# A graph-attention kernel's weighted sums: one accumulator instead of two, a reduce for a copy, and spread-out source rows in the empty slots

## The reference

```
for i in range(3):                       # layer 0: three hops
    Hn = segment_sum(H[src] * edge_weight, dst) @ Wn[i].T + bn[i]
    H  = elu(Hn + H @ Ws[i].T + bs[i])   # no elu on the last
x = layernorm(x + H)

h = x @ W.T                              # layer 1: attention, 8 heads of 32
alpha = <h[src], a_src> + <h[dst], a_dst> + <relu(edge_attr @ edge_W.T + edge_b), h[dst]>
alpha = where(alpha >= 0, alpha, 0.2 * alpha)
ex = exp(alpha - segment_max(alpha, dst)[dst])
attn = ex / max(segment_sum(ex, dst)[dst], 1e-10)
x = layernorm(x + segment_sum(h[src] * attn, dst) + bias)
```

## Time and profile before

| | us |
|---|---|
| median of three runs | 3030.04 (3027.95 to 3031.69) |
| the profiled execution, its time | 3030.28 |
| its span in the trace | 3028.5 |
| DVE busy | 1797.2 (59%) |
| POOL busy | 1846.8 (61%) |
| PE busy | 2444.8 (81%) |
| indirect gathers on POOL (L636), 416 of them | 403.3 |
| adds to the two accumulators (L1830), 208 and 208 | 424 and 423 ns each at the median |
| exp columns (L1836), 104 of them | 169 / 684 / 1917 ns at least, median, most |

### The profile page before, as it was taken

One profiled execution on the slowest core, in us unless ns is written; L12 is line 12 of the kernel. 1 busy time (PEld: TensorE's weight loads), 2 busy tenths in 40 slices (PEclk: granted clock), 3 DMA queues, 4 the chain that ended last, 5 costly groups with the idle time before them and its releaser, 6 DMA issues.

```text
span 3028.5 us, 46970 instructions
## 1 busy us (share of the span) xinstructions
PE 2444.8 (81%) x9398; PEld 1573.7 (52%) x9399; DVE 1797.2 (59%) x4277; ACT 1068.3 (35%) x3018; POOL 1846.8 (61%) x1738
## 2 busy tenths in 40 slices
PE   6999976477777779999899999999776667727772
PEld 5888843255555544445444454445555555525552
DVE  7765559899999940001344401113777777768888
ACT  1222221488888830000000000000333333347773
POOL 4777777777777760000067777760677777747774
PEclk9999979699989999999999999998888888869997
DMA  3000010355555564443344444442577777757772
GB/s 128 3 4 3 3 25 3 112 183 183 183 183 183 183 208 132 135 129 112 101 124 122 122 123 132 133 138 86 176 217 217 216 218 219 212 122 215 207 210 82
DMA packets 425651, 415.44 MB, mean 137 GB/s; under 512 B 85386, under 2 KB 411489, under 8 KB 424929
## 3 DMA queue, kind: packets, MB, share of 16 engines
q1 hardware_dynamic: 367681, 348.28, 37.0%
q0 software_dynamic: 57888, 66.23, 9.8%
HBM read 247.08 MB, written 167.17 MB: 137 GB/s over the span
## 4 chain that ended last, share of the span: by engine, by line
PE 50%; POOL 14%; issue 11%; SPq 8%; DVE 6%; DMA 4%; DVEq 3%; ACT 2%; ACTq 0%; POOLq 0%
PE psum L912 27%; POOL gath L636 9%; SPq L489 6%; PE psum L724 5%; POOL rows_by_pair L597 5%; PE psum L1028 4%; DVEq L405 3%; PE psum L709 3%; PE psum L904 2%; DMA gath<-gat_rows,rec 2%; PE psum L783 1%; PE psum L842 1%; SPq L483 1%; PE psum L700 1%; ACT lw L1099 1%
## 5 line engine op out<-in xcount | busy, mean ns | idle before, releaser
L622 POOL DMA_INDIRECT rows_by_dst<-rec,place x392 | 381.1, 972 | 533.4 <-DVE place L1457 405.8
L912 PE MATMUL psum<-a_t,acc 128*128 128x512 f32 (+1 forms) x1400 | 553.7, 551 | 0.0
L636 POOL DMA_INDIRECT gath<-gat_rows,rec x416 | 403.3, 969 | 215.4 <-issue 116.2
L607 POOL DMA_INDIRECT rows_by_low_digit<-rec,place x392 | 438.0, 1117 | 127.6 <-issue 127.6
L842 PE MATMUL psum<-rhot,lw 128*128 128x256 f32 x1440 | 381.2, 419 | 160.1 <-ACT lw L1099 126.5
L597 POOL DMA_INDIRECT rows_by_pair<-rec,place x392 | 386.5, 986 | 161.5 <-issue 126.6
L842 PEld LDWEIGHTS psum<-rhot,lw 128*128 128x128 f32 x1440 | 276.5, 206 | 264.9 <-ACT lw L1099 163.7
L912 PEld LDWEIGHTS psum<-a_t,acc 128*128 128x128 f32 x1400 | 257.7, 195 | 271.7 <-issue 267.9
L1565 DVE SCALAR_TENSOR_TENSOR merged<-merged,same_of,psum 128x256 f32<-128x256 f32 x720 | 310.0, 477 | 30.5 <-PE psum L842 18.7
L912 PE MATMUL psum<-a_t,x 128*128 128x512 f32 (+1 forms) x700 | 294.3, 549 | 0.0
L1099 ACT ACTIVATE lw<-lhot,recs_pair 128x128 f32<-128x128 bf16 x720 | 236.8, 387 | 94.8 <-DVE lhot L1548 83.0
(11 more groups left out here) (319 smaller groups left out, 3464.7 us busy)
## 6 DMA issues: line engine op xcount, KB each, us to landing
a_t<-adjacency SPq DMA_DIRECT2D x450, 256.0 KB, 2.7
adjacency<-merged SPq DMA_DIRECT2D x721, 128.0 KB
gat_h_by_edge<-gath SPq DMA_DIRECT2D x104, 528.0 KB, 4.1
gath<-gat_h_by_edge SPq DMA_DIRECT2D x104, 528.0 KB, 4.0
gath<-gat_rows,rec POOLq DMA_INDIRECT x416
rows_by_pair<-rec,place POOLq DMA_INDIRECT x392
rows_by_low_digit<-rec,place POOLq DMA_INDIRECT x392
rows_by_dst<-rec,place POOLq DMA_INDIRECT x392
```

The lines of the kernel that those rows point to most:

```text
L607: pool.indirect_dma_start(out=rows_low, in_=rec[:, c, :], out_offset=bass.IndirectOffsetOnAxis(ap=place[:, 1, c:c + 1], axis=0), in_offset ...
L622: pool.indirect_dma_start(out=rows_dst, in_=rec[:, c, :], out_offset=bass.IndirectOffsetOnAxis(ap=place[:, 0, c:c + 1], axis=0), in_offset ...
L636: pool.indirect_dma_start(out=gath[:, g % 4, c % 4, :], out_offset=None, in_=hh_dram, in_offset=bass.IndirectOffsetOnAxis(ap=rec_i[:, c, 0 ...
L912: i = pe.matmul(sums[b], table_g[:, w, b * P:(b + 1) * P], a_t[:, q % NA, 0:width(g)], start=False, stop=w == USED - 1)
```

## The change

Three edits. First, `zeros` gets in word 0 of each record the number 18 times the partition plus the slot, by an iota on POOL after the clearing, and SP's prefilling waits for that as well. Empty slots of both tables then name differing sources. Second, `exp_columns` makes the same values by `tensor_reduce` with a maximum over an axis of length one, in place of `tensor_copy`. Third, all adds go to `acc`; each waits for the add right before it; the final addition of `x0` is gone, and so is POOL's clearing of `x0` with the wait for `s_end` in front of it. POOL's clearing of `acc` now stands first there, behind its own wait for `s_loc`.

```diff
+PAD_STEP = 18
...
-            sp.wait_ge(s_fill, 1)
+            sp.wait_ge(s_fill, 2)
             sp.dma_start(rows_pair.rearrange("(p c) k -> p (c k)", p=P), zeros[:, :]).then_inc(s_fill, 16)
...
             pool.memset(zeros[:, :], 0.0).then_inc(s_fill, 1)
-
-            pool.wait_ge(s_fill, 1 + 32)
+            pool.wait_ge(s_fill, 1)
+            pool.iota(zeros[:, :].bitcast(I32).rearrange("p (c k) -> p c k", k=REC)[:, :, 0], [[1, NS]], base=0,
+                      channel_multiplier=PAD_STEP).then_inc(s_fill, 1)
+
+            pool.wait_ge(s_fill, 2 + 32)
             pool.wait_ge(s_rec, 6)
...
-            pool.wait_ge(s_end, 64)
-            nc.gpsimd.memset(x0[:, :, :], 0.0).then_inc(s_clr, 1)
             pool.wait_ge(s_loc, LOCAL * NB)
             nc.gpsimd.memset(acc[:, :, :], 0.0).then_inc(s_clr, 1)
...
             def add(n, k, w):
                 dve.wait_ge(s_mm, n + 1)
-                if not (isinstance(n, int) and n < 2):
-                    dve.wait_ge(s_add, n - 1)
-                a = (acc, x0)[k % 2][:, bass.ds(w, 1), :].rearrange("p c d -> p (c d)")
+                if not (isinstance(n, int) and n == 0):
+                    dve.wait_ge(s_add, n)
+                a = acc[:, bass.ds(w, 1), :].rearrange("p c d -> p (c d)")
                 v.tensor_tensor(a, a, bank[k][:, 0:HX], ALU.add).then_inc(s_add, 1)
...
             def exp_columns(g, q, first):
                 if not first:
                     dve.wait_ge(s_mm, 4 * (g - 3))
-                v.tensor_copy(val[:, q, :, D:HX], s_sb[:, bass.ds(4 * g, 4), :]).then_inc(s_vx, 1)
+                v.tensor_reduce(val[:, q, :, D:HX], s_sb[:, bass.ds(4 * g, 4), :].unsqueeze(3), X,
+                                ALU.max).then_inc(s_vx, 1)
...
-            dve.wait_ge(s_clr, 2)
+            dve.wait_ge(s_clr, 1)
...
             dve.wait_ge(s_add, NC)
-            v.tensor_tensor(acc[:, :, :], acc[:, :, :], x0[:, :, :], ALU.add).then_inc(s_add, 1)
-            dve.wait_ge(s_add, NC + 1)
             v.tensor_scalar(x0[:, :, D:HX], acc[:, :, D:HX], 1e-10, None, ALU.max).then_inc(s_ln, 1)
```

More of the change, by code:

```diff
@@ L73 @@
 ROWS_STORED = 2 * (NG - 1)
+assert (P - 1) * PAD_STEP + NS <= N
 assert EC % PIECE == 0 and PIECE % 4 == 0 and 0 < LAST < EC and EC % U == 0 and SEGS * SEGC == EC and SEGS % 2 == 0 and SEGC % MID == 0
```

## The result

The changed kernel takes 3117.44 us (median of 4, 3116.81 to 3119.62) against 3030.86 us in the same measurement: a ratio of 1.0288 (95% interval 1.0275 to 1.0302). The forecast was 3116. The span of the profiled execution is 3115.8 us against 3028.5, 87.3 us more. Nearly all of the loss is in the weighted sums (98.9 us); the maxima lose 3.4 more, and the merge and the last gathers give 15 back.

The account below looks back on a forecast made before the run. In the sums DVE waits only for its sequencer, and the window-number load hides the long copy. +96 − 7.3 − 7.3 + 4.7 = +86 us on 3030.3 gives 3116 us, range 3084 to 3134.

Parts of the forecast that it names:

- The chained adds: Weighted sums on DVE: adds waiting for their predecessor start every 0.635 us instead of 0.34; +96 us.
- The step that made the number: DVE's sequencer between adds: wait release 0.04, register operation 0.07 later, add 0.10 later; 0.21 us behind the predecessor's end.
- The lower forms that were bounds (0.46, 0.57): Chained adds' spacing in us: 0.46 with wait nearly free (rival, 0.06), 0.57 if the register operation carries it (0.11).
- The long copy: Exp columns in the sums: window-number load of 1.84 us hides the copy, so reduce gains 0; contrary rival's chance 0.04.
- Merge and slots: Merge behind the last add gone, −7.3 us; differing sources in empty slots, last gather earlier, −7.3 us.
- The clearing: POOL's clearing of acc moves beside scans over the ends and delays a DVE operation on the path: +4.7 us.
- the two ends named: Bounds on the moved clearing's cost on the path: 0 and 5.9 us.
- that case (3.2): Moved clearing catches only DVE's operation at 2678.70, not the copy at 2676.03: it ends 3.2 us late.
- The iota: Start, on POOL before the prefilling: 0.7 to 0.9 us while DVE waits 1.75 for edges; 0, at most +0.9.
- the last rival: PE's clock falls in the sums: +38 us at most, 3154; 0 to 5 us at a third of the time; chance 0.07.

Follow-up runs that it names:

- chain_only: Kernel before with one accumulator, each add waiting for the one right before, no merge, clearings unmoved: 4358.44 us against 4267.04 on another chip, ratio 1.0204.
- wait_only: Kernel before, both accumulators and merge kept, each add waiting for the one right before: 4370.24 us against 4267.04 on another chip, ratio 1.0239.
- one_wait: Changed kernel with PE waited for once per quad, by its first add: 3102.83 us, ratio 1.0246 to the kernel before; sums 351.4 us.
- reduce_only: Kernel before with exp columns by a reduce, nothing else changed: 4265.01 us against 4267.04 on another chip, ratio 0.9992; sums 267.5 us.

## Why the prediction was right

*The chained adds.* The step that made the number was to count what the sequencer does between an add's end and the next one's start, and it held: 0.21 us predicted, 0.21 measured, in rows of three kernels (`chain_only`, `wait_only` and the changed one). The three steps are there one by one: behind the add that ends at 2864.767 the separate wait instruction comes at 2864.805, the register operation at 2864.874 and the add at 2864.978, so 0.04, 0.07 and 0.10 us, as the prediction had put them together.

The size was short. In the middle of the loop 16 chunks take 14.27 us instead of 10.38, 3.89 more and not 3.69. Of the 0.20 us, about 0.08 is that an add that is no longer overlapped takes 0.430 and not 0.424 us (0.642 a step and not 0.635); 0.02 lies behind a short copy; 0.10 lies behind the two loads, where the prediction had 0.04 less and each distance grew by 0.03 (medians 2.41 to 2.44, 2.80 to 2.83). Over 26 steps that would be 5 us more than forecast; it is 2.9, since the start of the sums loses less. The first 28 adds take 4.3 us more than before, where the loop's pace would give 6.8; about 1 us of that is the reduce's.

The lower forms that were bounds (0.46, 0.57) are real too: `one_wait` has the 0.57, since there the register operation alone carries the wait, and 0.46 is the distance from the last add to the instruction behind it. As to the rule of the Trainium skill, "VectorE: DVE Perf Modes", section "The DRAIN you can't avoid", that a semaphore costs nothing between chained operations, the trace disagrees: `wait_only` changes no operation and no tile, only which add is waited for, and its sums take 100 us more.

*The long copy.* Right: `reduce_only` moves nothing but 1.0 us at the start of the sums. What the prediction did not see is the second cover, ACT. It had ACT at 3.9 us a turn, its busy time; where nothing else held it, with a step of 0.14 us in each quad, ACT took 4.07 us a turn (2 × 2.035).

*Merge and slots* were right within 0.4 us.

*The clearing.* The mechanism was right, the size between the two ends named: the second copy was not caught (it had begun at 2668.36, before the first was over, and the clearing seems to have got in only behind both); the one-input operation was. The loss on the path is 3.4 us and not 4.7, near the prediction's own figure for that case (3.2).

*The iota.* It cost nothing, but it was nearer than said. It took 1.63 us, not 0.7 to 0.9, and held two casts of DVE:

```profile
8.25 1.63 POOL L594 IOTA zeros<- 128x720 int32 x1
...
8.61 1.42 DVE L1267 CAST identb<-identf 128x128 bf16<-128x128 f32 x1
...
11.65 0.57 DVE L1280 CUSTOM_DVE_ANT_0 dst_i<-dst_i,pad_i 128x784 uint16<-128x784 uint16 x1 [0.41 <-DMA ea_in<-in_edge_attr]
```

Of DVE's 1.75 us of slack 0.41 are left.

*PE's clock* fell, from 0.99 to 0.91, as the last rival had it, and cost nothing: PE's busy time rose by 77 us inside a stage in which it waits for DVE anyway.

*The total* is nearer than its terms. The sums cost 2.9 us more than forecast, the clearing 1.3 and the slots 0.4 less; that these leave 1 us is luck. The mechanisms are not.

## What to carry to other kernels

Between short instructions that depend on one another, price the sequencer, not the engine: the wait's release, each separate wait instruction and each register operation stand between the end of one and the start of the next, and two independent chains hide them. Where an engine is stalled at a place, look first at what else its own queue does there; a faster instruction under a load of registers was worth 1 us of 269 here. Where several engines are nearly full, find the one whose steps never vary and whose end the others follow by a fixed distance. A wait taken away moves work earlier, and it matters what it then lies beside.

## What the runs showed of the hardware

- Waiting for the instruction just before cost an add of 264 elements on DVE, with a register operation in front of it, 0.30 us (0.34 to 0.64): 0.09 of lost overlap and 0.21 behind its end, of which a separate wait instruction is 0.07.
- Indirect reads of one row of device memory, 128 in a DMA, took 0.49 us a packet at the scores' end, differing rows 0.18.
- A clearing on POOL held a one-input float32 operation on DVE for 3.5 us, until 0.2 us behind its own end (0.36 to 3.82 us; 0.36 again with the clearing elsewhere), and was itself 0.65 us longer where it began beside two copies. Two-input operations between them kept their 0.57 to 0.58 us. An iota on POOL held two casts in the same way (0.21 to 1.42 and 1.48 us).
- Copies of 32 float32 elements on DVE beside POOL's products took up to 1.9 us and ended 0.035 to 0.039 us behind a product; the same elements by a reduce took 0.17 to 0.19 us.
- A load of registers from SBUF took DVE's sequencer 0.30, 0.52, 0.96 and 1.84 us for 1, 2, 4 and 8 numbers.
- One chip ran the kernel before 41% slower than the others, with stalls marked "remote" ahead of the sums and none in them. Why stays open.
